# Selective scan: the product with C written over the states, one ring of four steps instead of rings of three and two

## The reference, cut to what matters

```python
def step(h, inp):
    d_t, u_t, b_t, c_t = inp
    dA = jnp.exp(d_t[..., None] * A)
    h = dA * h + (d_t * u_t)[..., None] * b_t[:, None, :]
    y_t = jnp.einsum('bdn,bn->bd', h, c_t)
    return (h, y_t)
```

## Time and profile before

| | before |
|---|---|
| median of the runs | 3416.22 us |
| profiled execution, time | 3414.18 us |
| its span, first to last instruction | 3412.4 us |
| VectorE busy | 2371.1 us (69%) |
| GpSimd busy | 1702.9 us (50%) |
| ScalarE busy | 1819.3 us (53%) |
| TensorE matmuls busy | 2663.4 us (78%) |
| mean granted TensorE clock | 0.86 |

### The profile page before, as it was taken

How to read it: one execution, slowest core, us unless ns; L and a number is a source line. 1 busy time by engine, 2 the same in 40 slices (tenths; PEclk the granted TensorE clock), 3 DMA queues, 4 the chain that set the end, 5 groups by cost and what they waited for, 6 DMA issues and landing times. The chain is left out here.

```text
span 3412.4 us, 36441 instructions
## 1 busy us (share of the span) xinstructions
PE 2663.4 (78%) x10431; PEld 1545.8 (45%) x10432; DVE 2371.1 (69%) x2860; ACT 1819.3 (53%) x2980; POOL 1702.9 (50%) x636
## 2 busy tenths in 40 slices
PE   5766776676676667657667438999999999999997
PEld 2222222122122122212212115888888888888886
DVE  2999999899999899999999964333334334344443
ACT  3657666666666666666666534444444444444442
POOL 0888888898898888888888850000000000000000
PEclk8777877788787787778878657999999999999999
DMA  3344433444433444334444322000000000000000
GB/s 89 80 99 111 111 94 88 104 105 99 107 93 91 105 111 100 91 94 105 99 111 98 88 85 97 13 13 12 13 12 13 12 13 12 13 12 13 12 13 13
DMA packets 138266, 225.74 MB, mean 66 GB/s; under 512 B 14432, under 2 KB 49120, under 8 KB 138080
## 3 DMA queue, kind: packets, MB, share of 16 engines
q1 hardware_dynamic: 138080, 223.80, 26.4%
HBM read 173.42 MB, written 50.33 MB: 66 GB/s over the span
## 5 line engine op out<-in xcount | busy, mean ns | idle before, releaser
L753 DVE TENSOR_TENSOR_SCAN h<-bank,state,db 128x512 f32<-128x512 f32 x1024 | 1255.9, 1273 | 84.6 <-POOL hc L630 61.0
L630 POOL TENSOR_TENSOR hc<-h,c_rows 128x2048 f32<-128x2048 f32 x256 | 1159.2, 4533 | 85.1 <-DVE h L753 48.8
L560 ACT ACTIVATE bank<-d_bc,a_neg 128x512 f32<-128x512 f32 x1024 | 699.1, 687 | 595.0 <-DVE h L753 594.0
L955 PE MATMUL s_bank<-s_act,weights_r 128*128 128x512 f32 x4096 | 935.0, 389 | 0.0
L955 PEld LDWEIGHTS s_bank<-s_act,weights_r 128*128 128x128 f32 x4096 | 767.8, 188 | 158.6
L1117 DVE TENSOR_TENSOR s_act<-s_h,s_act 128x512 fp32r<-128x512 f32 x384 | 262.8, 689 | 638.0 <-ACT s_act L1053 625.1
L388 PE MATMUL bank<-bc,w_spread 64*128 64x512 f32 x272 | 157.3, 602 | 449.4 <-DVE db L738 445.7
L1076 ACT ACTIVATE s_h<-s_bank,s_sc 128x512 f32<-128x512 f32 x256 | 176.0, 687 | 528.8 <-PE s_bank L955 528.6
L738 DVE TENSOR_TENSOR db<-bank,du_bc 128x2048 f32<-128x2048 f32 x192 | 436.5, 2273 | 19.8 <-DMA du_bc<-du_rows 19.8
L409 PE MATMUL bank<-hc,fold_w 128*32 128x512 f32 x2048 | 358.9, 782 | 93.5 <-DVE uz L777 78.0
L388 PEld LDWEIGHTS bank<-bc,w_spread 64*128 64x128 f32 x272 | 59.4, 232 | 658.1 <-DVE db L738 571.3
(11 more groups left out here) (91 smaller groups left out, 2304.1 us busy)
## 6 DMA issues: line engine op xcount, KB each, us to landing
d_bc<-d_rows SPq DMA_DIRECT2D x256, 256.0 KB, 4.4
du_bc<-du_rows SPq DMA_DIRECT2D x256, 256.0 KB, 7.5
d_rows<-sp_r SPq DMA_DIRECT2D x64, 256.0 KB, 2.0
du_rows<-sp_w SPq DMA_DIRECT2D x64, 256.0 KB, 2.0
xT_sb<-in_xT SPq DMA_DIRECT2D x16, 512.0 KB, 9.0
x_nat<-in_x SPq DMA_DIRECT2D x16, 512.0 KB, 4.6
x<-res SPq DMA_DIRECT2D x16, 512.0 KB, 3.2
s_x_nat<-x SPq DMA_DIRECT2D x16, 512.0 KB, 4.4
```

Source lines behind the costliest of these rows:

```text
L560: act.activation(decays[DECAY_BANK[g]][:], d_bc[c % 2][:, j, :], ACT.Exp, scale=a_neg[:, g:g + 1]).then_inc(decay, 1)
L630: pool.tensor_tensor(hc[:, k % HCSTEPS], h[:, H_SLOT[k]], c_rows[:, q, :].unsqueeze(1).broadcast_to([P, JC, NT]), ALU.mult).then_inc(hc_do ...
L753: dve.tensor_tensor_scan(h[:, H_SLOT[k], j, :], decays[DECAY_BANK[g]][:], db[:, k % DBSTEPS, j, :], state[:, g:g + 1], ALU.mult, ALU.add). ...
L955: last = pe.matmul(dst, weights[:, w_at + k * rows_w + cols:w_at + k * rows_w + cols + P], ins[j][:, k, :], start=k == 0 and j == 0, stop= ...
```

## The change

The buffer `hc` goes. GpSimd writes its product with C over the states in `h`, and `h` gets four slots, so that step `k` always uses slot `k % 4`. TensorE folds out of `h`. GpSimd may overwrite a step's states only when ScalarE has saved their last column, so `times_c` now waits for `saved` of its own step, and no longer for TensorE. The first scan of a step waits for the fold of the step four back. In a step the remaining waits are the same.

```diff
-HSTEPS, DBSTEPS, HCSTEPS = 3, 2, 2
+HSTEPS, DBSTEPS = 4, 2
...
-H_SLOT = [k % HSTEPS if k < NK - 1 else 1 for k in range(NK)]
...
-        hc = sb("hc", [P, HCSTEPS, JC, NT])
...
                 for j in range(JC):
-                    last = pe.matmul(p_y[GD * j:GD * j + GD, :], fold_w[:], hc[:, k % HCSTEPS, j, :],
+                    last = pe.matmul(p_y[GD * j:GD * j + GD, :], fold_w[:], h[:, k % HSTEPS, j, :],
                                      start=q == 0, stop=q == QN - 1, tile_position=(0, GD * j))
...
                 src = (zeros[:, 0:JC] if t.tt == TILES_B - 1 else
-                       h[:, H_SLOT[k], :, NT - 1:NT].rearrange("p a b -> p (a b)"))
+                       h[:, k % HSTEPS, :, NT - 1:NT].rearrange("p a b -> p (a b)"))
...
-                pool.wait_ge(folded, t.count(NK, k - HCSTEPS + 1 + FOLDED0))
-                pool.tensor_tensor(hc[:, k % HCSTEPS], h[:, H_SLOT[k]],
+
+                pool.wait_ge(saved, t.count(NK, k + 1 + SAVED0))
+                pool.tensor_tensor(h[:, k % HSTEPS], h[:, k % HSTEPS],
                                    c_rows[:, q, :].unsqueeze(1).broadcast_to([P, JC, NT]), ALU.mult).then_inc(hc_done, 1)
...
-                    before = holder_before(H_SLOT, k)
-                    dve.wait_ge(saved, t.count(NK, before + 1 + SAVED0))
-                    dve.wait_ge(hc_done, t.count(NK, before + 1 + HC0))
-                dve.tensor_tensor_scan(h[:, H_SLOT[k], j, :], decays[DECAY_BANK[g]][:], db[:, k % DBSTEPS, j, :],
+                    dve.wait_ge(saved, t.count(NK, k - NK + 1 + SAVED0))
+                    dve.wait_ge(folded, t.count(NK, k - HSTEPS + 1 + FOLDED0))
+                dve.tensor_tensor_scan(h[:, k % HSTEPS, j, :], decays[DECAY_BANK[g]][:], db[:, k % DBSTEPS, j, :],
                                        state[:, g:g + 1], ALU.mult, ALU.add).then_inc(scanned, 1)
```

More of the change, by code:

```diff
@@ L210, in mamba_stage @@
         N_NEWTON = 7
-        DECAY0, SCANNED0, SAVED0, HC0, FOLDED0, DVE0, POOL0, OUT0 = 2 * GC, 2 * JC, NK, QN, HCSTEPS, 2 * QV, 2, SUB + 1
+        DECAY0, SCANNED0, SAVED0, HC0, FOLDED0, DVE0, POOL0, OUT0 = 2 * GC, 2 * JC, NK, QN, HSTEPS, 2 * QV, 2, SUB + 1
         COPIES = 16 * GN
```

## The result

The changed kernel takes 3454.55 us, the median of four runs (3453.87 to 3457.88), beside 3416.28 us for the kernel before on the same chip. The ratio is 1.0113, with a 95% interval of 1.0101 to 1.0126: 38 us slower. The prediction was 3456 us. The profiled execution has a span of 3452.1 us, 39.7 more than before.

What follows compares the result with a forecast made beforehand. VectorE was taken to set the pace, busy 1818 of the state-space stage's 2031 us. Terms +6 + 32 + 1 + 1 = +40 us on 3414.18 gave 3454, as median 3456 us, 1.2% slower; range 3430 to 3485.

Steps and rivals of the forecast that it cites:

- part 1: First scan of step 15: the 3.80 us ring stall goes, but ScalarE leaves only 1.4 us a tile.
- the SiLU piece: ScalarE's long piece ahead of the decay of group 63; waits for nothing of VectorE's, so limits the ring gain to 1.4 us.
- part 2: Saves of steps 14 and 15 delay GpSimd's products and the transfer for step 4; with part 1, +6 us.
- The wake-up: Time from the end of a save to the start of GpSimd's product it releases, taken as 0.15 us.
- part 3: Save of step 7 delays GpSimd's product 4.2 us; VectorE stalls 2.1 us a tile at step 12; +32 us in sum.
- The chain: From the end of `sp_w` to VectorE's product that needs the transfer: 12.7 us, read from the last tile.
- part 4: Other steps: late saves are hidden or taken up by GpSimd's idle time ahead of its `db` product; +1 us allowed.
- some 30 waits at L737: Sign in the profile after: VectorE waits for `du_bc` some 30 times, 1.8 to 2.5 us each, at steps 12 and 4.
- parts 5, 6: TensorE: GpSimd's 29.4 us fold wait goes but gives nothing; writing in place: 0 to 2 us, taken as 1.
- The transfers are hidden: Rival: no transfer stalls, only part 1's 1.4 us a tile count, 21 us gained, 3395 us; chance 0.07.
- GpSimd becomes the bound: Rival: the 4.2 us delay at step 7 reaches VectorE whole, 73 us slower, 3489 us; chance 0.08.

Runs made afterwards that it cites:

- e2: The kernel before with four slots for the states, separate buffer for the product with C and fold wait kept: 3393.89 us, ratio 0.9933.
- e7: e2 without ScalarE's SiLU of z and its table loads, for timing only: 3367.13 us, ratio 0.9853.
- e4a: The changed kernel with GpSimd's softplus products ahead of the product with C in chunk 3 alone: 3425.31 us, ratio 1.0025.
- e5: The changed kernel with softplus products ahead of the product with C in chunks 1, 2 and 3, and ScalarE's save one place earlier: 3397.33 us.
- e11: e2 with GpSimd's product with C also waiting for the save of its own step: 3455.08 us, ratio 1.0116.
- e4: The changed kernel with GpSimd's softplus products ahead of the product with C in chunks 1, 2 and 3: 3397.39 us, ratio 0.9944.

## Why the prediction was right

**The ring stall** (part 1) went whole, and ScalarE gave most of it back: 3.8 us a tile gone, 2.65 us a tile at the softplus line in e2, where 0.2 were before. I took 1.4 us a tile as the net gain, 21 us in all; e2 measured 22. That the SiLU piece is the cause was shown by e7. In the changed kernel the stall at step 0 (below) stands in the place of ScalarE's piece, at nearly the same price: 35.0 + 5.2 us, where e2 has 0.2 + 39.0.

**The wait for the save at steps 14 and 15** (part 2) made the product of step 4 wait as forecast: 1.8 us forecast, 23.7/15 = 1.6 measured. The wake-up I took at 0.15 us is 0.08 in the rows.

**The wait at step 7** (part 3) was forecast as 2.1 us at step 12 and measured as 32.1/16 = 2.0. Less the 4.6 us that were there before, that is 27.5. With the 2.3 us that the first scan of step 11 waits in the last tile, which was forecast too (part 3 gave that tile 3.6 in all), it is 30 of the 32 us forecast. e4a shows its price by itself: with the wait at step 12 down by 25.5 us, it is 29 us faster than the changed kernel. The chain that the term hangs on, 12.7 us from `sp_w` to the product with B, came out as 12.65 in the median of 31 stalls, though single ones run from 12.2 to 13.7. The Trainium skill (DMA: Bandwidth & Descriptors, on the anatomy of one DMA) would have had 9.4, by the estimate in the prediction; the trace doesn't agree, and by that estimate neither stall would exist.

**The other steps** (part 4): one thing there was wrong. I wrote that GpSimd's idle time takes up what is late at the other steps, and left out step 11. Its save is late too, its softplus products stand behind it, and the product of step 0 waits 35.0/15 = 2.3 us in each tile. Before the change the chain had 4.1 us to spare there (median, by a chain of 12.65 us), but 3.8 of these were the ring stall itself, which lies between; in e2, with the stall gone, 0.2 us are left. The total came out right all the same, since this stall lies in the shadow of ScalarE's piece: e5 took it away for 0.1 us. That was luck, as I hadn't looked for it. So the forecast of some 30 waits at L737 was low: 49 were counted, 37 and 12, the kernel's first among them.

**TensorE and the in-place write** (parts 5, 6): no gain and no cost. I had allowed 1 us for the write; e11 shows none.

**The sum** was 40 us and so is the measurement, but its terms miss by a few us each way. The stall at step 4 came out 3 us below the 27 that part 2 has for it, and part 3 was 2 too high. Against that, VectorE's busy time grew by 4.0 us and scans waited 1.7 us more, where I had allowed 2 in all. No run shows what made VectorE's busy time longer. That the total is within 2 us of the forecast is in part chance.

**The rivals.** "The transfers are hidden", 3395 us, is what e2 and e4 show, 3394 and 3397 us. So its size was right and its condition false. "GpSimd becomes the bound" didn't come: its idle time ahead of the product with B fell to 21.7 us, but scans waited only 1.3 us for it by name and at most 4.0 with the waits that have no name.

## What to carry to other kernels

When a wait is added to an instruction, its price is not read from what the instruction feeds but from what is queued behind it. Here no scan waited for the late product with C once the ring had four slots, while the two small products behind it start chains of transfers that had 1 to 2 us to spare at steps 4, 8 and 12; putting them ahead of the wait turned 38 us lost into 19 gained. Slack behind a stall must be counted again once the stall goes. And a stall that is removed is worth only the distance to the next engine's limit at that place, so look at what that engine does there before counting the whole.

## What the runs showed that I had not expected

An instruction of GpSimd started 0.08 us after the end of the ScalarE instruction that released it, in the four places shown. GpSimd's product of 128x2048 takes the same time in place (4527 ns) as into another buffer (4529 in e11, 4533 before), although in the kernel before the two in-place products of 128x512 take 1284 and 1275 ns and the one into another buffer 1268. And a chain of one store and eight transfers of 256 KB on one queue took 12.65 us in the median at two places of the tile, and 12.72 in the last tile of the kernel before.
